# Two-part f16 probabilities in latent attention, and a second evacuation on VectorE

## The reference, cut to what matters

```python
q_r = jnp.einsum('bshq,hqr->bhsr', q_big, W_qr)
k_r = jnp.einsum('bld,hdr->bhlr', kv_r, W_kr)
scores = jnp.einsum('bhsr,bhlr->bhsl', q_r, k_r)
attn = jax.nn.softmax(scores, axis=-1)
ctx_c = jnp.einsum('bhsl,bld->bhsd', attn, kv_r)      # the product that the change rewrites
ctx_lat = jnp.einsum('bhsd,hkd->bhsk', ctx_c, w_kc_kv)
```

## Time and profile before

| | |
|---|---|
| median of 3 runs | 531.78 us (531.44 to 533.56) |
| the profiled execution's own time | 531.13 us |
| its span, first to last instruction | 529.4 us |
| PE busy | 490.2 us, 93% |
| VectorE busy | 321.7 us, 61% |
| ScalarE busy | 245.5 us, 46% |
| GpSimd busy | 182.1 us, 34% |
| mean granted clock of TensorE | 0.973 |

### The profile page before, as it was taken

One profiled execution on the slowest core, in us unless ns is written; L12 is line 12 of the kernel. 1 busy time (PEld: TensorE's weight loads), 2 busy tenths in 40 slices (PEclk: granted clock), 3 DMA queues, 4 the chain that ended last, 5 costly groups with the idle time before them and its releaser, 6 DMA issues. The chain is left out here.

```text
span 529.4 us, 9451 instructions
## 1 busy us (share of the span) xinstructions
PE 490.2 (93%) x3202; PEld 345.2 (65%) x3202; DVE 321.7 (61%) x881; ACT 245.5 (46%) x596; POOL 182.1 (34%) x181
## 2 busy tenths in 40 slices
PE   4988989987789999999999999999989879999997
PEld 2776878775336566556656565656766546999986
DVE  4989799732477677676867676675465790322102
ACT  3674364643026666566666667656634300332200
POOL 3141311302157566665666566674410000000000
PEclk9997999999699999999999999999989979999999
DMA  8813000000000020202001000000069000087002
GB/s 266 230 55 92 2 1 1 1 1 1 0 1 1 2 71 0 72 0 56 13 14 55 0 0 0 0 1 1 2 163 285 1 1 1 21 260 228 2 0 80
DMA packets 41298, 26.25 MB, mean 50 GB/s; under 512 B 10048, under 2 KB 40816, under 8 KB 41264
## 3 DMA queue, kind: packets, MB, share of 16 engines
q1 hardware_dynamic: 41264, 25.81, 16.8%
HBM read 24.75 MB, written 1.05 MB: 49 GB/s over the span
## 5 line engine op out<-in xcount | busy, mean ns | idle before, releaser
L1055 POOL TENSOR_TENSOR PB<-PB,inv 128x512 f32<-128x512 f32 x64 | 66.5, 1039 | 89.8 <-DVE inv L1117 89.3
L990 ACT ACTIVATE PB<-ps,low 128x256 f32<-128x256 f32 x128 | 59.6, 471 | 48.0 <-DVE low L1111 48.0
L1111 DVE TENSOR_REDUCE low<-ps 128x2 f32<-128x512 f32 x64 | 43.9, 685 | 31.6 <-PE ps L904 30.8
L1082 DVE TENSOR_TENSOR TM<-ps,cosq 96x512 f32<-96x512 f32 x64 | 43.9, 686 | 22.6 <-PE ps L882 21.1
L882 PE MATMUL ps<-XH,CH 128*96 128x512 f16 x128 | 49.8, 389 | 2.7 <-POOLq L1042 2.6
L882 PE MATMUL ps<-XL,CH 128*96 128x512 f16 x128 | 49.5, 387 | 0.0
L882 PE MATMUL ps<-XH,CL 128*96 128x512 f16 x128 | 49.5, 387 | 0.0
L1049 POOL TENSOR_TENSOR RO<-TM 96x512 f32<-96x512 f32 x32 | 40.5, 1267 | 21.4 <-DVE TM L1083 21.4
L1083 DVE TENSOR_TENSOR TM<-ps,sinq 96x512 f32<-96x512 f32 x64 | 43.3, 677 | 0.0
L912 PE MATMUL ps<-ident,PB 128*128 128x128 f32 x256 | 40.6, 281 | 1.8 <-POOL PB L1055 1.1
L358 POOL TENSOR_TENSOR HT<-GL,MS 128x512 f32<-128x512 f32 x16 | 20.3, 1277 | 63.6 <-ACT MS L630 48.7
(11 more groups left out here) (220 smaller groups left out, 973.3 us busy)
## 6 DMA issues: line engine op xcount, KB each, us to landing
EG<-in_L_ffn_W_gate_dram SPq DMA_DIRECT2D x10, 384.0 KB, 4.3
EU<-in_L_ffn_W_up_dram SPq DMA_DIRECT2D x10, 384.0 KB, 5.1
ED<-in_L_ffn_W_down_dram SPq DMA_DIRECT2D x10, 384.0 KB, 5.7
w<-in_L_ffn_W_dram SPq DMA_DIRECT2D x2, 1024.0 KB, 8.5
WQ<-in_L_xattn_Wq_dram SPq DMA_DIRECT2D x8, 256.0 KB, 2.8
WO<-in_L_xattn_Wo_dram SPq DMA_DIRECT2D x8, 256.0 KB, 3.1
WCQ<-in_L_xattn_w_kc_q_dram SPq DMA_DIRECT2D x8, 192.0 KB, 2.7
X<-in_x_dram SPq DMA_DIRECT2D x2, 512.0 KB, 4.1
```

The source lines that it names most:

```text
L990: e = act.activation(PB[t % 2][:, h, :], g.ps[:, SC + t % 2, h * S:(h + 1) * S], ACT.Exp, bias=low[:, t % 2, h:h + 1], scale=-1.0, accum_o ...
L1055: pool.tensor_tensor(PB[t % 2][:, :, :], PB[t % 2][:, :, :], inv[:, t % 2, :].unsqueeze(2).broadcast_to([P, 2, S]), ALU.mult).then_inc(nor ...
L1082: dve.tensor_tensor(batches(TM[st % 2][:, c, :]), src, over(g.cosq[:, a, :]), ALU.mult)
L1111: dve.tensor_reduce(low[:, t % 2, :], g.ps[:, SC + t % 2, :].rearrange("p (h s) -> p h s", h=2), AX.X, ALU.min).then_inc(low_ok, 1)
```

## The change: what it does

The latents are also kept as two f16 parts, KVP, made by GpSimd in the first stage. The turned probabilities leave PTB twice: ScalarE writes 256 times their value as f16 and signals t_hi; VectorE then subtracts that from 256 times PTB and writes the low f16 part, and it is VectorE that signals t_ok. An attend takes three f16 products (high by high, high latents by low probabilities, low latents by high probabilities) for each of its four f32 ones, 12 matmuls for 4. The factor 256 is taken out where the attended context is copied and where its low part is made. VectorE's `turned` of tile t - 2 stands behind tile t's minimum; its fold remainder, `to_context` and `inverse` come after it, and the rotations and `attended` behind the inverse.

```diff
@@ first stage, GpSimd, behind KV's second copy
+                pool.tensor_copy(g.KVP[:, 0, :, :], g.KV[:, :, 0, :]).then_inc(kvp_ok, 1)
@@ behind the loop that writes XA, ahead of the folds' second parts
+                pool.wait_ge(kvp_ok, 1)
+                pool.tensor_tensor(g.KVP[:, 1, :, :], g.KV[:, :, 0, :], g.KVP[:, 0, :, :],
+                                   ALU.subtract).then_inc(kvp_ok, 1)
@@ attention
-        PTS = two("PTS", [P, 4, 2 * P])
+        PTS = two16("PTS", [P, 2, 4, 2 * P])
@@ PE, attend
                     for j in range(2):
-                        for h in range(2):
-                            mm = pe.matmul(g.ps[DC * h:DC * h + DC, CXB, 0:S], g.KV[:, 2 * b + j, 0, :],
-                                           PTS[b % 2][:, 2 * h + j, :], start=(j == 0), stop=(j == 1))
+                        for m, (kv, part) in enumerate(((0, 0), (0, 1), (1, 0))):
+                            for h in range(2):
+                                mm = pe.matmul(g.ps[DC * h:DC * h + DC, CXB, 0:S], g.KVP[:, kv, 2 * b + j, :],
+                                               PTS[b % 2][:, part, 2 * h + j, :], start=(j == 0 and m == 0),
+                                               stop=(j == 1 and m == 2))
@@ ScalarE, turned and attended
-                    act.activation(PTS[t // 2 % 2][:, :, (t % 2) * P:(t % 2 + 1) * P],
+                    act.activation(PTS[t // 2 % 2][:, 0, :, (t % 2) * P:(t % 2 + 1) * P],
                                    g.ps[:, PTB, :].rearrange("p (j n) -> p j n", j=4),
-                                   ACT.Copy).then_inc(t_ok, 1)
+                                   ACT.Copy, scale=UPP).then_inc(t_hi, 1)
@@
-                                   ACT.Copy).then_inc(cx_hi, 1)
+                                   ACT.Copy, scale=1.0 / UPP).then_inc(cx_hi, 1)
@@ VectorE, attended
-                    dve.tensor_tensor(g.XCL[:, bass.ds(p, 1), cols], g.ps[:, CXB, 0:S],
-                                      g.XCH[:, bass.ds(p, 1), cols], ALU.subtract).then_inc(cx_ok, 1)
+                    dve.scalar_tensor_tensor(out=g.XCL[:, bass.ds(p, 1), cols], in0=g.ps[:, CXB, 0:S],
+                                             scalar=1.0 / UPP, in1=g.XCH[:, bass.ds(p, 1), cols], op0=ALU.mult,
+                                             op1=ALU.subtract).then_inc(cx_ok, 1)
@@ VectorE, new
+                def turned(p, t):
+
+                    dve.wait_ge(t_hi, 8 * p + (t + 1))
+                    cols = slice((t % 2) * P, (t % 2 + 1) * P)
+                    dve.scalar_tensor_tensor(out=PTS[t // 2 % 2][:, 1, :, cols],
+                                             in0=g.ps[:, PTB, :].rearrange("p (j n) -> p j n", j=4), scalar=UPP,
+                                             in1=PTS[t // 2 % 2][:, 0, :, cols], op0=ALU.mult,
+                                             op1=ALU.subtract).then_inc(t_ok, 1)
@@ VectorE, step
                     lowest(p, t)
+                    if t >= 2:
+                        turned(p, t - 2)
+                    if folds and t in (4, 5):
+                        fold(p + 2, u, t - 4)
                     if t == 2:
                         to_context(p, u, 1)
                     if t == LAST and asks:
                         to_context(p + 1, 1 - u, 0)
-                    if folds and t in (4, 5):
-                        fold(p + 2, u, t - 4)
+                    inverse(p, t)
                     if asks:
                         rotate(p + 1, t)
                     if t in (4, 6):
                         attended(p, t // 2 - 2)
-                    inverse(p, t)
@@ VectorE, cross
                     lowest(p, t)
+                    turned(p - 1, NT - 2 + t)
+                    inverse(p, t)
                     if asks:
                         rotate(p + 1, t)
                     if t == 0:
                         attended(p - 1, B - 2)
-                    inverse(p, t)
-                    if t == 0 and folds:
-                        fold(p + 1, 1 - u, FOLDS - 1)
-                    if t == 1:
+                        if folds:
+                            fold(p + 1, 1 - u, FOLDS - 1)
+                    else:
                         attended(p - 1, B - 1)
@@ VectorE, behind the pairs
+                turned(PAIRS - 1, NT - 2)
                 attended(PAIRS - 1, B - 2)
+                turned(PAIRS - 1, LAST)
                 attended(PAIRS - 1, B - 1)
```

More of the change, by code:

```diff
@@ L115 @@
 UPW = 256.0
+UPP = 256.0
 def split(ah, al, bh, bl):
@@ L257, in stage_first_layer @@
         d_w1, d_w2, d_wr, d_br, d_sh = map(sem, ["d_w1", "d_w2", "d_wr", "d_br", "d_sh"])
-        id_zero, id_ok, kv_mul, kv_sum, kv_ok, lg_fill = map(
-            sem, ["id_zero", "id_ok", "kv_mul", "kv_sum", "kv_ok", "lg_fill"])
+        id_zero, id_ok, kv_mul, kv_sum, kv_ok, kvp_ok, lg_fill = map(
+            sem, ["id_zero", "id_ok", "kv_mul", "kv_sum", "kv_ok", "kvp_ok", "lg_fill"])
         filled, hi_ok, emptied, at_ps = map(sem, ["filled", "hi_ok", "emptied", "at_ps"])
@@ L824, in stage_latent_attention @@
         (q_ps, rope_ok, sum_ok, qc_ps, qc_ok, s_ps, low_ok, exp_ok, inv_ok, norm_ok, t_ps, t_ok, cx_ps, cx_ok,
-         fold_ps, fold_ok, credit, fold_hi, qc_hi, cx_hi) = map(sem, [
+         fold_ps, fold_ok, credit, fold_hi, qc_hi, cx_hi, t_hi) = map(sem, [
              "q_ps", "rope_ok", "sum_ok", "qc_ps", "qc_ok", "s_ps", "low_ok", "exp_ok", "inv_ok", "norm_ok",
              "t_ps", "t_ok", "cx_ps", "cx_ok", "fold_ps", "fold_ok", "credit", "fold_hi", "qc_hi",
-             "cx_hi"])
+             "cx_hi", "t_hi"])
         EXP0, ROPE0, TPS0, TOK0, CXPS0, CXOK0, QC0, QCPS0, SUM0, FOLD0 = 2, 2, 2, 1, 2, 1, 1, 2, 4, 1
@@ L1697, in build @@
             g.KV = mb("KV", [P, NT, 2, DC])
+            g.KVP = mb("KVP", [P, 2, NT, DC], F16)
             g.KH, g.KL = mb("KH", [P, T], F16), mb("KL", [P, T], F16)
```

## The result

The change makes the kernel slower: 556.82 us (median of 4 runs, 553.59 to 557.53) against 531.61 (4 runs, 529.66 to 533.56), a ratio of 1.046 [1.041, 1.052]. The prediction, 550, had the direction; the measured time is 0.8 us above the top of its range. The profiled execution took 556.33 us with a span of 554.6, at a mean granted clock of 0.965 (0.973 before).

A forecast was written before the change was run, and what follows sets the result against it. PE's queue was taken to set attention's pace. Pairs 0 to 5 12.4, loop turns 0.6, pair 6 2.5, pair 7 1.4 and the end 1.2 made 18.1 us on 531.13: 549.2, plus 0.65 for the median, 550 us; range 542 to 556.

The forecast's parts named there:

- Second tile's turn: PE's turn of tile 1 in step 2 waits for VectorE's low part of tile 0: 0.53 us late.
- Third tile's attend: PE's attend of batch 0 in step 3 waits for tile 1's low part: 1.50 us late, less 0.21 saved.
- Folds: PE's second and third fold products, steps 4 and 5, wait for VectorE's fold remainder behind the low part: 0.60 us each.
- Half of it: Rival, chance 0.12: waits of steps 2 and 3 occur, those of the folds do not; 543 us.
- The gain arrives: Rival, chance 0.07: VectorE's low part is never late and the attends' 6.7 us saving stays; 525 us.
- The f16 products one after another: Rival, chance 0.05: the two heads' f16 products do not run side by side, 20 us on top; 570 us.
- VectorE the bound throughout: Rival, chance 0.04: VectorE's work and waits feed each other with the held PE, period may be 33; about 560 us.
- no other stage moved: Sign expected in the changed profile: stages outside attention keep their time.
- the last two pairs and the end: Pair 6 2.5 us, pair 7 1.4, and turn and attend at the end of attention 1.2.
- in idle time: The inverse, moved ahead of the rotations, waits some 0.45 us for ScalarE's exponentials, within VectorE's idle time.
- Each period, +2.07: One pair of heads: 1.29 + 0.60 + 0.60 - 2 x 0.21 us; pairs 0 to 5 give 12.4.
- the loop's turns: After a turn of the loop VectorE starts the minimum 0.3 us later, now on the path: 2 x 0.3 = 0.6.

The follow-up runs named there:

- the products alone: Changed kernel with no low part made, its product reading the high part again, t_ok from ScalarE and VectorE's queue as before: 523.66 us, ratio 0.985.
- the other three moves: Changed kernel with fold remainder first, context parts in tile 3, tile 2's minimum and tile 0's low part ahead of the last attended part: 544.65 us.
- the fold's move: Changed kernel with VectorE's fold remainder ahead of its low part in tiles 4 and 5: 551.77 us, ratio 1.038.
- the context parts': Changed kernel with VectorE's two context parts moved from tile 2 to tile 3, behind tile 1's low part: 552.63 us, ratio 1.040.
- several moves together: Changed kernel with fold remainder first, context parts later, tile 2's minimum and tile 0's low part earlier, inverse behind the rotations: 538.62 us, ratio 1.015.
- hoisted kernel: Changed kernel with tile 2's minimum and tile 0's low part ahead of the pair before's last attended part: 552.79 us, ratio 1.040.
- two-product kernel: Changed kernel without the probabilities' low part, two products per attend, t_ok from ScalarE, VectorE's queue as before: 523.68 us, ratio 0.986.

## Why the mechanism was right, and where the sum was too small

**The mechanism: right.** It said that VectorE is idle enough on average and late at four places. These are the places, with the same releaser. Second tile's turn: PE idle 0.63; the prediction has it as 0.53 late and 0.21 of gained time, 0.74. Third tile's attend: 1.11, against 1.50 late less the 0.53 that the turn had already put everything off, 0.97. Folds: 0.55 and 0.55 for 0.60 each.

**The new instruction: right.** 680 ns on average for the 0.69 taken from the 96x512 row. ScalarE's copy of the turned block costs what it did, 596 ns for 598, and GpSimd's two new instructions 0.61 and 1.15 us.

**The attends: right on PE.** 0.78 us from the attend's first record to the turn's (266.61 to 267.39) for 0.80; before 1.01. The two heads' f16 products run side by side. The Trainium skill's rule ("TensorE: Matmul & The Clock Gate", Part 3) that a load overlaps only matmuls of another row group is not borne out here: twelve loads of 109 ns each, 1.3 us of loads, lie within that 0.78 and overlap the matmuls, and with the products alone the kernel is faster. Of the 6.7 us that were to come from it only 4.8 arrived without the evacuation, and 5.5 beside it (277.70 - 272.24).

**The evacuation of PSUM.** The products give 4.8 us and the second reading of the turned bank takes 26.8. The Trainium skill, "TensorEngine Tiling (Array Packing)", PSUM Bottleneck, warns that the way out of PSUM may become the bottleneck once TensorE's part is faster. The products alone don't show that here: with the old way out, attention got 4.8 us shorter, and PE's new waits are for GpSimd. The loss comes from more work on the way out. The Trainium skill's page also advises using ScalarE and VectorE both for it: here both read the same whole bank, one behind the other, instead of sharing it, so the step got longer; no run here shows them sharing it.

**The rivals.** *Half of it* is out, since both folds' waits are there. *The gain arrives* is what the kernel without the low part shows, 523.66 for the 525 worked out; in the change itself the place on which it turned, the start of tile 2's minimum, did not move earlier against the scores. *The f16 products one after another* is out by the 0.78. *VectorE the bound throughout* had 4 in 100 and a period of 33; the period is 32.3 and VectorE sets the pace in part of it only, which the next point takes up.

**The step that failed: the sum, in terms put at nothing or too low.** The profiled execution took 556.3 us where the sum gave 549.2, so 7.1 us are missing: 3.9 outside attention, which "no other stage moved" had at nothing; 1.9 in the last two pairs and the end; 1.3 in the rest of attention, where the inverse's wait was put "in idle time". Attention alone, at 21.3 for 18.1, would have left the time inside the range. That the median lies outside it by 0.8 us is also chance: the same kernel again gave 554.78, which is inside.
- *Each period, +2.07.* The five periods from the last fold product of pair 1 on take 161.58 us, 32.32 each, against 149.67, 29.93: +2.39. With the loop's turns (0.6 over the run, some 0.12 a period) the prediction had 2.19. The rest, 0.2 a period, is small; but the reason that was given for leaving it out is wrong. The prediction put the inverse's wait for the exponentials "in idle time". Here is the stretch that holds tiles 2 to 5 (length, busy of PE, PEld, DVE, ACT, POOL, clock, DMA):

```profile
257.00:275.50 18.50, 15.66 (x114) 10.24 (x114) 16.37 (x32) 10.94 (x33) 10.17 (x10) 1.00 0.13 35
...
275.50:289.00 13.50, 13.38 (x92) 8.22 (x90) 10.09 (x19) 8.38 (x23) 7.90 (x7) 1.00 0.06 14
```

In the first stretch VectorE is busy for 16.37 of 18.50 us, 88%, and PE for 85%; in the second VectorE for 75% and PE for 99%. In the first there is little idle time to hide a wait in. The runs show that the moved inverse cost time: putting it back gave 0.27 us a period by itself and 0.92 on top of the other three moves. The four waits are not independent either: the fold's move gave 0.58 us a period for the 1.2 of its two waits, the context parts' 0.17, because the work that was put off was met a tile later.
- *The last two pairs and the end, predicted at +5.1 (2.5 + 1.4 + 1.2): +6.99* (53.00 to 59.99). From attend to attend, pair 6 lost 3.5 us for 2.5, pair 7 2.5 for 1.4, and the end 1.0 for 1.2. Pair 6 has no folds, so PE comes to the attend sooner and waits 1.68 instead of 1.11. In pair 7 the first turn and attend wait 0.47 and 0.80, where 0.25 a tile was estimated. At the end turn and attend wait one after the other:

```profile
406.63 0.63 PE L918 MATMUL ps<-ident,PB 128*128 128x128 f32 x4 [1.50 <-DVE PTS L1132]
...
408.67 0.85 PE L928 MATMUL ps<-PTS,KVP 128*64 128x256 f16 x12 [1.41 <-DVE PTS L1132]
```

against 0.78 and 0.69: +0.72 each, for 0.73 predicted.
- *The start of attention, to the same product of pair 1, +2.42* (48.25 to 50.67), for a period's 2.07.
- *"No other stage moved": +3.9.* PE's busy time there is 3.6 us longer for the same matmuls. Here is the profile's clock in one stretch of the first layer, before, then after:

```profile
35.00:55.00 20.00, 16.95 (x93) 13.20 (x92) 18.86 (x77) 9.55 (x22) 4.43 (x5) 0.83 0.33 92
```

```profile
35.00:55.00 20.00, 16.12 (x75) 12.24 (x71) 17.36 (x71) 8.57 (x19) 4.01 (x5) 0.74 0.34 92
```

The granted clock is 0.74 for 0.83. Behind attention, in equally long stretches of the experts, it is 0.91 before (388 to 407 us) and 0.85 after (411 to 430). Over the profiles of all kernels of this case the time outside attention goes from 275.7 us (mean clock 0.980) to 282.7 (0.962), whatever was edited in attention. GpSimd's two instructions alone moved the median by nothing that can be told. In two later profiles, GpSimd's instructions alone in the kernel before and the changed kernel again, it is 281.4 and 280.6. The two kernels with the shortest time outside attention, 275.7 and 277.0, have GpSimd's instructions too. So most of the 3.9 is matmuls at a lower clock, and GpSimd's instructions aren't its cause. Whether the change brings the lower clock about is not settled, since no run isolates it. The medians differ by 25.2 us and attention by 21.3 to 22.5, so some 3 us stay open.

## What to carry to other kernels

A mean busy share of 61 or 66% says nothing about an engine that is busy for 88% of a stretch of 18.5 us in a period of 32.3: look at its share in the stretch between two of its forced waits, and count each added instruction there at full price. An added evacuation of a single PSUM bank costs its own time plus its place in that queue, so weigh it against what the products in front of it save before splitting them. Waits along such a stretch are not worth their lengths one by one: a single move shifts most of a wait to the next place (0.17 to 0.58 us a period here), and several moves together give more than their sum (2.20 for 1.22). So try the order as a whole: here it gave back two thirds of the loss, and halving the added work 9.3 us. And compare stages by stretches that repeat: the periods agreed between two profiles of one kernel to 0.01 us, the stage as a whole only to 1.2.

## What the runs showed of the hardware that was not expected

**An idle PE and the clock.** In the hoisted kernel PE stood idle for 2.01 us ahead of the attend at 362.25; the attend then took 1.37 us instead of 0.85, the turn 1.11 instead of 0.66, and a 128x256 f16 record 0.42 instead of 0.27. The windows around it (clock in the third column from the right):

```profile
355.00:362.00 7.00, 5.07 (x36) 3.12 (x32) 6.61 (x12) 3.82 (x10) 4.58 (x4) 1.00 0.01 2
```

```profile
362.00:366.00 4.00, 3.75 (x22) 2.69 (x23) 2.00 (x5) 1.64 (x6) 2.91 (x3) 0.57 0.00 0
```

The granted clock fell from 1.00 to 0.57 of full speed, close to the lower of its two levels (1.2 of 2.4 GHz), and was back at 1.00 in the window from 366. In the changed kernel a wait of 1.11 us had no such sequel (clock 1.00 from 257 to 275.5), nor had the one of 1.68 in pair 6, whose attend took 0.84. From the attend's start to the first query behind it took 3.07 us (362.25 to 365.32), where the same sequence took 1.69 two tiles earlier (354.56 to 356.25). So a wait can cost more than its length, here 1.4 us more. All three moves together, whose wait at this attend is 0.60, show no such thing.

The end of attention shows it too. There the last turn and attend wait 1.50 and 1.41 us, one behind the other, where the kernel before waits 0.78 and 0.69. In all ten profiles of kernels in which VectorE signals t_ok, the granted clock between the last attend and the end of attention is 0.78 or less; in the four in which ScalarE does, it is 1.00. When in this stretch the clock fell differed even between the two profiles of the changed kernel, and that is worth the 1.1 us by which their attention differs. That the longer waits bring it about is likely by these profiles, but no run varies them alone.

**Column halves in f16.** Twelve records of 128x256 with 64-wide weights and as many loads take 0.78 us to the next turn's first record, eight take 0.56 (two-product kernel, 260.11 to 260.67), so 0.055 us for each further record, half of the 0.11 between starts of a record that has the array to itself.

**The evacuation's price by columns.** VectorE's scaled subtraction from PSUM to f16 takes 680 ns for 512 columns and 412 for 256 (medians), from which about 1.05 ns a column and 144 ns fixed follow, an estimate from two sizes; for the fold's 384 columns it gives 546, and 0.55 us is in the earlier trace rows.
